# Both shared experts ahead of the slot blocks, and the next group's maxima three steps earlier

## The reference, cut to what matters

```python
# third layer: 2 shared experts on every token, 8 routed ones, 2 per token
x = x + _L0_ffn_ref(_layernorm(x), g_shared, W1_s, b1_s, W2_s, b2_s,
                    g_routed, W1_r, b1_r, W2_r, b2_r, centroids)
# fourth layer: 16 heads of 16, keys and values from ctx_1024, masked
x = x + _L1_xattn_ref(_layernorm(x), ctx_1024, mask, Wq, bq, Wkv, bkv, Wo, bo)
# an expert: h = gelu(xn @ W1 + b1), 256 -> 1024; out = h @ W2 + b2, 1024 -> 256
```

## Time and profile before

| | us |
|---|---|
| median of 3 timed runs | 2180.64 |
| lowest and highest | 2177.63, 2182.57 |
| the profiled execution | 2199.48 |
| its span, first to last instruction | 2197.7 |
| its mean granted TensorE clock | 0.898 of 2.4 GHz |

### The profile page before, as it was taken

How to read it: one execution, slowest core, us unless ns; L and a number is a source line. 1 busy time by engine, 2 the same in 40 slices (tenths; PEclk the granted TensorE clock), 3 DMA queues, 4 the chain that set the end, 5 groups by cost and what they waited for, 6 DMA issues and landing times.

```text
span 2197.7 us, 35268 instructions
## 1 busy us (share of the span) xinstructions
PE 1771.0 (81%) x14036; PEld 971.9 (44%) x14036; DVE 1385.8 (63%) x2137; ACT 1064.1 (48%) x1834; POOL 465.0 (21%) x347
## 2 busy tenths in 40 slices
PE   7988948878787888755999999999994678937866
PEld 5566635545555777441333333333333234623433
DVE  2231264260174999768999999999936665147556
ACT  3221113666543666410998989899892015211510
POOL 2322133676422666520000000000002000020000
PEclk9998969998977999985999999999996788978968
DMA  7113011777614555326425343342100721054100
GB/s 284 59 57 130 1 39 51 227 229 233 218 41 154 177 206 190 91 49 98 91 53 96 62 77 81 62 95 53 43 2 5 86 30 40 1 86 49 40 0 20
DMA packets 134880, 198.15 MB, mean 90 GB/s; under 512 B 20886, under 2 KB 100136, under 8 KB 130476
## 3 DMA queue, kind: packets, MB, share of 16 engines
q1 hardware_dynamic: 133052, 191.56, 34.8%
q0 software_dynamic: 1664, 4.33, 0.6%
HBM read 144.55 MB, written 50.99 MB: 89 GB/s over the span
## 4 chain that ended last, share of the span: by engine, by line
PE 35%; issue 29%; DVE 17%; SPq 8%; DMA 5%; POOL 3%; ACT 3%; DVEq 0%; ACTq 0%; POOLq 0%
SPq L754 5%; PE bank L1143 3%; PE pair L1484 3%; DVE w_lo L1924 3%; PE pair L1176 3%; DVE mx L2193 2%; PE bank L999 2%; PE bank L248 2%; DVE mx_part L2103 2%; DVE hid_lo L2005 2%; PE bank L1388 2%; PE bank L1043 1%; DMA xT<-x_slots 1%; PE pair L1338 1%; PE bank L306 1%
## 5 line engine op out<-in xcount | busy, mean ns | idle before, releaser
L1653 ACT ACTIVATE pexp_all<-bank 128x512 f32<-128x512 f32 x1024 | 552.4, 596 | 113.3 <-PE bank L1293 101.7
L2103 DVE TENSOR_REDUCE mx_part<-pair 128x2 f32<-128x1024 f32 x512 | 585.6, 1214 | 28.7 <-PE pair L1265 26.5
L1279 PE MATMUL bank<-pexp_all,vst 128*17 128x256 f32 x4096 | 323.1, 388 | 5.6 <-issue 5.5
L1265 PE MATMUL pair<-kst,qs 49*128 49x512 f16 x1024 | 209.6, 406 | 61.2 <-DVE mx_part L2103 28.7
L1293 PE MATMUL bank<-qs,kst 52*128 52x256 f16 x2048 | 203.4, 272 | 2.1 <-DMA qs<-prt_rows 2.0
L1265 PEld LDWEIGHTS pair<-kst,qs 49*128 49x128 f16 x1024 | 50.0, 93 | 288.7 <-DVE mx_part L2103 196.7
L1293 PEld LDWEIGHTS bank<-qs,kst 52*128 52x128 f16 x2048 | 118.6, 95 | 61.9 <-ACT pexp_all L1653 18.5
L1663 ACT ACTIVATE pexp_all<-pair 128x1024 f32<-128x1024 f32 x64 | 65.5, 1023 | 151.1 <-PE pair L1408 149.6
L2453 POOL TENSOR_SCALAR neg_grp<-mx_grp 128x8 f32<-128x8 f32 x16 | 3.7, 232 | 618.7 <-DVE mx_grp L2123 618.7
L1279 PEld LDWEIGHTS bank<-pexp_all,vst 128*17 128x17 f32 x4096 | 68.8, 95 | 114.8 <-issue 107.9
L1176 PE MATMUL pair<-w_hi,hid_hi 128*128 128x256 f16 x368 | 103.2, 281 | 11.2 <-issue 6.6
(11 more groups left out here) (313 smaller groups left out, 3449.3 us busy)
## 6 DMA issues: line engine op xcount, KB each, us to landing
w_f<-in_w_all SPq DMA_DIRECT2D x34, 1024.0 KB, 5.9
kst<-k_scr SPq DMA_DIRECT2D x192, 128.0 KB
v_scr<-v_st SPq DMA_DIRECT2D x64, 272.0 KB, 2.6
vst<-v_scr SPq DMA_DIRECT2D x16, 1088.0 KB, 6.1
ctx_sb<-in_ctx SPq DMA_DIRECT2D x16, 1024.0 KB, 4.9
cT<-in_ctxT SPq DMA_DIRECT2D x32, 512.0 KB, 4.5
k_scr<-k_hi SPq DMA_DIRECT2D x128, 64.0 KB, 2.6
k_scr<-k_lo SPq DMA_DIRECT2D x128, 64.0 KB, 2.3
```

Of the source, the lines that this page charges most:

```text
L1265: last = pe.matmul(pair[n % 2][:, e * 512:(e + 1) * 512], qs[g % NBK][rws, p, qt * P:(qt + 1) * P], kst[g % NBK][rws, p, kb * 512:(kb + 1) ...
L1279: last = pe.matmul(bank[3][32 * h:32 * h + HV, 0:S], vst[g % 2][:, c, h * HV:(h + 1) * HV], unit_exp[n % NUE][:, p * S:(p + 1) * S], start ...
L1653: act.activation(unit_exp[n % NUE], bank[SCORE_BANKS[n % 3]], ACT.Exp, scale=SCALE).then_inc(s_exp, 1)
L2103: dve.tensor_reduce(mx_part[:, :, 2 * p + qt, kb], pair[n % 2][:, :].rearrange("p (e k) -> p e k", e=2), X_AXIS, ALU.max).then_inc(s_mx, 1)
```

## The change

Jobs 0 and 1 are now the two shared experts and jobs 2 to 16 the 15 blocks. All tables and counts that hang on this move: the order of the halves, the blocks' slots, the semaphore counts, and which halves POOL helps with. Job 1's halves are loaded with job 0's, before the routing is known, and POOL makes low pieces of them (three) before the scatter. Behind the last block comes no further job. MAX_STEP is 20 in place of 23.

```diff
         def shared(q):
-            return q in (0, JOBS - 1)
+            return q < ES
...
-        HALVES = [(0, 0), (0, 1), (1, 0), (2, 0), (1, 1)]
-        for q in range(2, JOBS - 1):
+        HALVES = [(0, 0), (0, 1), (1, 0), (1, 1), (2, 0), (3, 0), (2, 1)]
+        for q in range(3, JOBS - 1):
             HALVES += [(q + 1, 0), (q, 1)]
...
-            return () if half in ((1, 0), (2, 0), (1, 1)) else (0,) if half[1] else (0, 1)
+            return () if half in ((2, 0), (3, 0), (2, 1)) else (0,) if half[1] else (0, 1)
...
-        MAX_STEP = 23
+        MAX_STEP = 20
...
             load_weights(0, 0)
             load_weights(0, 1)
+            load_weights(1, 0)
+            load_weights(1, 1)
             sp.wait_ge(s_route, EXPERTS)
-            load_weights(1, 0)
             load_weights(2, 0)
-            load_weights(1, 1)
+            load_weights(3, 0)
+            load_weights(2, 1)
             sp.wait_ge(s_xs, 16 * 2 * T)
-            load_block(1)
             load_block(2)
-            for q in range(1, JOBS - 1):
-                if q + 2 <= JOBS - 1:
+            load_block(3)
+            for q in range(2, JOBS):
+                if q + 2 < JOBS:
                     load_weights(q + 2, 0)
-                if q + 2 <= NBLK:
                     load_block(q + 2)
-                if q >= 2:
+                if q >= 3:
                     store_block(q - 1)
-                load_weights(q + 1, 1)
-            store_block(NBLK)
+                if q + 1 < JOBS:
+                    load_weights(q + 1, 1)
+            store_block(JOBS - 1)
...
             second_layer(0)
             turn_gates()
-            turn_block(1)
-            for q in range(1, NBLK + 1):
-                if q + 1 <= NBLK:
+            first_layer(1)
+            second_layer(1)
+            turn_block(2)
+            for q in range(2, JOBS):
+                if q + 1 < JOBS:
                     turn_block(q + 1)
                 first_layer(q)
-                if q >= 2:
+                if q >= 3:
                     second_layer(q - 1)
-            second_layer(NBLK)
-            first_layer(JOBS - 1)
             second_layer(JOBS - 1)
...
             for t in range(T):
                 take_shared(0, t)
-                if t == 5:
-                    weights_low((1, 0))
-            weights_low((2, 0))
-            weights_low((1, 1))
+                if t in (3, 5):
+                    weights_low((1, t // 4))
             for t in range(T):
                 n = out_tiles(0) + t
                 dve.wait_ge(s_w2, n + 1)
                 dve.wait_ge(s_acc, t + 1)
                 dve.tensor_tensor(u[:, t, :], u[:, t, :], out_of(n), ALU.add).then_inc(s_acc, 1)
-            block_low(1)
+            hidden_parts(1, range(2 * HM))
+            for t in range(T):
+                take_shared(1, t)
+                if t == 3:
+                    weights_low((2, 0))
+            weights_low((3, 0))
+            weights_low((2, 1))
+            block_low(2)
...
             for s_ in range(BLK // P):
-                take_block(NBLK, s_)
-            weights_low((JOBS - 1, 1))
-            hidden_parts(JOBS - 1, range(2 * HM))
+                take_block(JOBS - 1, s_)
             dve.wait_ge(s_ga, 16 * 2 * T)
...
-                take_shared(JOBS - 1, t)
-                dve.wait_ge(s_acc, out_before(JOBS - 1) + t + 1)
                 dve.tensor_tensor(x[:, t, :], x[:, t, :], u[:, t, :], ALU.add).then_inc(s_x, 1)
...
             weights_low((0, 0))
             weights_low((0, 1))
+            weights_low((1, 0))
+            weights_low((1, 1))
             pool.wait_ge(s_route, PLACED)
```

More of the change, by code:

```diff
@@ L782, in load_weights @@
             def load_weights(q, h):
-                if q == 0 or q == JOBS - 1:
-                    one = bass.ds(ER + (1 if q else 0), 1)
+                if shared(q):
+                    one = bass.ds(ER + q, 1)
                 else:
-                    e = sp.value_load(expert_of[0:1, q - 1:q], min_val=0, max_val=ER - 1)
+                    e = sp.value_load(expert_of[0:1, q - 2:q - 1], min_val=0, max_val=ER - 1)
                     one = bass.ds(e, 1)
@@ L800, in load_block @@
             def load_block(q):
-                if q >= 3:
-                    sp.wait_ge(s_xt, q - 2)
-                sp.dma_start(xb[q % 2][:, :, :], x_slots[(q - 1) * BLK:q * BLK, :].rearrange("(s p) n -> p s n", p=P))\
+                if q >= 4:
+                    sp.wait_ge(s_xt, q - 3)
+                sp.dma_start(xb[q % 2][:, :, :], x_slots[(q - 2) * BLK:(q - 1) * BLK, :].rearrange("(s p) n -> p s n", p=P))\
                     .then_inc(s_xbl[q % 2], 16)
@@ L808, in store_block @@
                 sp.wait_ge(s_acc, out_before(q) + out_tiles(q))
-                sp.dma_start(y_slots[(q - 1) * BLK:q * BLK, :].rearrange("(s p) n -> p s n", p=P), yb[q % 2][:, :, :])\
+                sp.dma_start(y_slots[(q - 2) * BLK:(q - 1) * BLK, :].rearrange("(s p) n -> p s n", p=P), yb[q % 2][:, :, :])\
                     .then_inc(s_ys[q % 2], 16)
@@ L1151, in first_layer @@
                 elif not shared(q):
-                    pe.wait_ge(s_xl, KT * q)
+                    pe.wait_ge(s_xl, KT * (q - 1))
                 for job in range(hidden_jobs(q)):
@@ L1210, in turn_block @@
             def turn_block(q):
-                pe.wait_ge(s_xbl[q % 2], 16 * ((q + 1) // 2))
-                if q >= 2:
-                    pe.wait_ge(s_xl, KT * (q - 1))
+                pe.wait_ge(s_xbl[q % 2], 16 * (q // 2))
+                if q >= 3:
+                    pe.wait_ge(s_xl, KT * (q - 2))
                 for k in range(KT):
@@ L1601, in block_high @@
             def block_high(q):
-                act.wait_ge(s_xt, q)
+                act.wait_ge(s_xt, q - 1)
                 for k in range(KT):
@@ L1613, in _ @@
             weights_high(1, 0)
-            weights_high(2, 0)
             weights_high(1, 1)
@@ L1618, in _ @@
                 act.activation(gateT[:, j * 512:(j + 1) * 512], src[0:ER + ES, :], ACT.Copy).then_inc(s_gTe, 1)
-            block_high(1)
-            for q in range(1, NBLK + 1):
-                if q + 1 <= NBLK:
+            hidden(1)
+            weights_high(2, 0)
+            weights_high(3, 0)
+            weights_high(2, 1)
+            block_high(2)
+            for q in range(2, JOBS):
+                if q + 1 < JOBS:
                     block_high(q + 1)
                 hidden(q)
-                if q >= 2:
+                if 3 <= q < JOBS - 1:
                     weights_high(q + 1, 0)
@@ L1627, in _ @@
             weights_high(JOBS - 1, 1)
-            hidden(JOBS - 1)
             act_dev(act, norm3)
@@ L2019, in take_block @@
                 dve.wait_ge(s_w2, n + 1)
-                if q >= 3 and s_ == 0:
-                    dve.wait_ge(s_ys[q % 2], 16 * ((q - 1) // 2))
+                if q >= 4 and s_ == 0:
+                    dve.wait_ge(s_ys[q % 2], 16 * (q // 2 - 1))
                 dve.tensor_scalar(yb[q % 2][:, s_, :], out_of(n), 1.0 / W_SCALE, None, ALU.mult).then_inc(s_acc, 1)
             def block_low(q):
-                dve.wait_ge(s_xh, KT * q)
+                dve.wait_ge(s_xh, KT * (q - 1))
                 for k in range(KT):
@@ L2057, in _ @@
                 dve.tensor_tensor(u[:, t, :], u[:, t, :], out_of(n), ALU.add).then_inc(s_acc, 1)
-            block_low(1)
-            for q in range(1, NBLK + 1):
-                if q + 1 <= NBLK:
+            hidden_parts(1, range(2 * HM))
[6 more added lines that the diff above has]
+            block_low(2)
+            for q in range(2, JOBS):
+                if q + 1 < JOBS:
                     block_low(q + 1)
                 hidden_parts(q, range(HM))
-                if q >= 2:
-                    weights_low((q + 1, 0))
+                if q >= 3:
+                    if q + 1 < JOBS:
+                        weights_low((q + 1, 0))
                     take_block(q - 1, 0)
@@ L2424, in _ @@
                                             in_=tok[:, t, :], in_offset=None).then_inc(s_xs, 16)
-            for q in range(2, NBLK + 1):
+            for q in range(3, JOBS - 1):
                 weights_low((q + 1, 0))
@@ L2429, in _ @@
             for i in range(2):
-                pool.wait_ge(s_ys[i], 16 * ((NBLK + i) // 2))
-            low_parts_done(pool, (NBLK, 1))
+                pool.wait_ge(s_ys[i], 16 * ((NBLK + 1 - i) // 2))
+            low_parts_done(pool, (JOBS - 2, 1))
             for t in range(T):
```

## The result

| | before | after |
|---|---|---|
| median, us | 2180.43 (4 runs) | 2202.15 (4 runs) |
| lowest and highest | 2177.63, 2182.57 | 2196.84, 2205.26 |
| the profiled execution | 2199.48 | 2201.96 |

The change makes the kernel slower by 21.7 us: the ratio is 1.0098, with a 95% interval of 1.0075 to 1.0121. The forecast was +15.6 (2196, range 2181 to 2211). The profiled executions differ by 2.5 us only, mainly because the one of before holds the stalls beside the indirect DMAs and the one of after holds none. That became the main question of the study.

A forecast was written before the change was run, and what follows sets the result against it. No single bound: TensorE busy 81% of 2197.7 us, VectorE 63%, each dense elsewhere. Terms 1 to 3 (+25.4) less 17.1 gave +8.3; without the 7.3 us stall in the timed kernel before, +15.6, 2196 us; range 2181 to 2211.

The forecast's parts named there:

- term 5: Stalls beside indirect DMAs burden only the profile, so moving the last shared expert saves 7.3 us less: +15.6, 2196 us.
- Term 1: Start of the expert stage: a second shared expert before the first block adds its layers, +43.3 us.
- Term 2: End of the blocks: the last block no longer waits for its weight halves before its second layer, -5.2 us.
- Term 3: Tail behind the last block: store, gather and adding stand uncovered but the shared expert is gone, -12.7 us.
- Term 4: Cross attention: MAX_STEP 20 removes the wait for the maxima's rows once per group, -17.1 us.
- rival C: Cross attention keeps its group period because another wait replaces the rows': 2210 us, chance 0.10.
- Rival B: The stalls beside the indirect DMAs are real in every run and stay: +8.3 us, 2189 us, chance 0.20.
- rival A: Weight loads cause the stall beside the scatter; fewer loads end it, timed runs too: 14.7 us back, 2174, chance 0.13.

The follow-up runs named there:

- Run 12: Kernel before with MAX_STEP 20, loads ahead of the stores, POOL making two of four low pieces of second halves, no memsets; 2164.9 us on chip 14, ratio 0.9949.
- Run 6: Changed kernel with the last half's load (job 16, second layer) issued ahead of the store of block 14; 2207.9 us, ratio 1.0017 to before.
- Run 7: Changed kernel gathering only each token's first result, 8 indirect DMAs and not 16; 2205.1 us, ratio 1.0003 to before.
- Run 2: Kernel before with MAX_STEP 20 in place of 23, nothing else; 2180.3 us on chip 3, ratio 0.9916.
- run 1: Kernel before, unchanged, profiled and timed again on chip 3; 2200.7 us, ratio 1.0013, profiled execution 2195.6 us.
- run 8: Kernel before with a POOL memset after each of the scatter's 16 DMAs, on chip 3; one execution of 2199.4 us, not used as a time.
- the experts' part alone: Changed kernel with MAX_STEP put back to 23, on chip 3; 2230.0 us, ratio 1.0127 to before.
- run 5: Changed kernel, unaltered, timed and profiled again beside before on chip 3; 2217.4 us, ratio 1.0050 to before.

## Why the prediction was right, and where it wasn't

**The sign and the mechanism** were right: a shared expert's whole time comes in front, what it covered comes out, and the maxima give back half. The forecast of +15.6 rests on term 5 as well, and there the reason was wrong; that its number still fitted the timed runs was luck.

**Term 1, +43.3.** Run 12 shows the old start without a stall (from job 0's first product to the end of its second layer 47.7 us, as in after): 61.0 us from job 0's first product (626.24) to the first block (687.26). After it is 106.0 (630.79 to 736.77): +45.0. The bias products and the pieces came out within 0.6 us of their terms. The first layer was under-sized, 23.1 and not 20.7: I took the last shared expert's rate, but here PE comes out of the transposes and bias products with waits between them, the granted clock is 0.67 in 680 to 690, and the first products start some 0.43 us apart, which is the lower level (1.2 GHz), where they start 0.216 apart at the higher (2.4 GHz). The second was over-sized, 21.1 and not 22.3. The extra loads and POOL's three pieces cost nothing, as forecast; the scatter starts at 664.7, 34.0 us behind job 0's first product where it was 31.1, so 2.8 later (forecast 2), and PE never waits for it.

**Term 2, -5.2.** This step failed by half. From the first block to the last the stage takes 198.7 us and took 201.1: -2.4. I wrote that ACT made the halves without a wait for the load and would make them "by 891.9 at the latest". With less to do ACT got there before the load, which SP issues only after a store that waits for block 14's output. Run 6 gave the missing part back, and more: 192.4 us from the first block to the last.

**Term 3, -12.7.** Measured -13.1 (54.5 us without PE against 67.6 from 903.2 to 970.8). By its pieces: 3.4 to POOL's first DMA (forecast 3.45), 19.8 for sixteen (20.4), 1.8 to landing (1.45), 13.7 for the adding (13.9). The Trainium skill's rule (DMA: Bandwidth & Descriptors, "Anatomy of one DMA") gave an estimate of 2.3 for the landing; the trace, from the end of POOL's last instruction to DVE's start, has 1.8 and decides. Much of the -13.1 is the stall in the gather, see the sum. Run 7 confirms the pace.

**Term 4, -17.1.** Run 2 measured -18.5 (5.7 to either side), its profile 17.9. The rival C, that the period stays, is refuted by it.

**Term 5.** The arithmetic was right for runs without the stall, the reason wrong. I took the stalls for a burden of the profile. On chip 3 a profiled execution is no longer than the timed ones (run 1), all seven profiles with dense DMAs show the stall in the scatter, and before is 20 to 27 us slower there than on chips 8 and 14 and in the first comparison. The one profile of dense DMAs from chip 14 (run 12) and the one of after show none; from chip 8 there is no profile of a dense scatter. So the stall goes with where the kernel runs. That before's first profile, with its stall, came from another chip than its timed runs at 2180 is my inference; the record doesn't say. Rival B, real stalls, gave +8.3, and chip 3 measured +11.0 (6.2 to 16.1).

The sign that I had named for rival A came true, a second layer of job 0 of 22 us in the profile, but not its time of 2174: a timed kernel before that had no stall left nothing to gain. A named the loads as the cause. Run 12 had the same loads (share 0.50, 184 GB/s) without a stall, after had more (0.73, 246), and run 8 ran through on chip 3 itself at 199. The rule of the Trainium skill behind it (Runtime: NRT & Kernel Launch, "Instruction fetch mechanics") isn't borne out either: in the stall, 664 to 679, the traces of before and run 1 have no packet of instructions under way, and those of run 12 and after, without a stall, have one in the same stretch.

**The sum.** By my terms 45.0 - 2.4 - 13.1, and 7.3 for the stall that the timed kernel before didn't have, less 17.1 to 18.5, is +18.3 to +19.7, against 21.7 with an interval of 16.4 to 26.4. The 7.3 was sized too small. Run 12 gathers with dense DMAs and without a stall:

```profile
893.00:914.00 21.00, 21.00 (x101) 9.67 (x99) 18.03 (x33) 10.50 (x16) 13.50 (x14) 1.00 0.31 91
```

Its last shared expert takes 41.8 us, where before's took 50.3, and from its last block to the transposes (L248) lie 59.1 us, not 67.6. So the stall was worth 8.5, the tail alone -4.6, and the sum is +19.5 to +20.9. The miss of 6.1 is term 2 (2.8), term 1 (1.7), this stall (1.2) and what the interval leaves open.

## What to carry to other kernels

Work that seems to stand idle at a stage's end may be the cover of a slow transfer: before moving it, cost what comes out from under it. When an engine is relieved, look at the queue that feeds it, since a load behind an unrelated store is late next. Two edits with opposite signs hide each other: the maxima alone were worth -18.5 us, the experts' part alone +28.0.

## What the runs showed of the hardware

- Beside indirect DMAs 1.27 us apart, PE issues a step in some 1.4 us on chip 3, and runs at full rate on chip 14 and in after's profile; run 5 and after are the same program. At 1.84 us apart chip 3 doesn't stall, in the one execution that was made. In chip 3's profiles the stall lengthens job 0's second layer by 10 to 15 us. Before's timed runs are 20 to 27 us longer there; that the stalls make up most of this is inferred. What differs between the chips was not found, and no chip but 3 and 14 has a profile on record that can tell.
- The stall begins 8 to 11 us after the scatter's first DMA, not with it (664.6 for a scatter from 656.0 in before). Why was not tested.
- In every profile PE's granted clock has an early stretch of 17 us at the lower level, while PE is busy, and where it falls differs with the same program. In four of the fourteen it begins at 82 to 83 us, in three at 143 and in seven at 202 to 203. After's profile is one of the four, before's one of the seven; the same window of each, after and then before:

```profile
80.00:96.00 16.00, 14.72 (x55) 11.48 (x56) 1.94 (x5) 0.00 (x0) 0.00 (x0) 0.58 0.15 62
```

```profile
80.00:96.00 16.00, 15.03 (x111) 12.83 (x111) 7.13 (x9) 1.66 (x2) 0.00 (x0) 1.00 0.09 35
```

The granted clock is 0.58 in the one and 1.00 in the other, and PE was busy for the same 64.5 to 64.6 us of the 80 before. The products that follow (L963, before the change L961) start at 100.66 and at 92.08, of which 7.2 us come from this stretch; at job 0's first product after is 5.9 us behind. Two single executions of this kernel can't be compared to better than this; places have to be compared from a common instruction on.
